# A mixture-of-experts block on one core: the fetched rows of the later tiles transposed by VectorE in 32x32 pieces

## The reference

```python
logits = jnp.einsum('bsd,ed->bse', x, router_w)
topk_vals, topk_idx = jax.lax.top_k(jax.nn.softmax(logits, axis=-1), 2)
for eid in range(8):
    w = jnp.sum(jnp.where(idx == eid, vals, 0), axis=-1)
    h = jax.nn.gelu(x_flat @ w1[eid].T, approximate=False)   # 256 -> 1024
    out = out + w[:, None] * (h @ w2[eid].T)                 # 1024 -> 256
```

## Time and profile before

| | us |
|---|---|
| time, median of 3 runs | 585.92 (585.22 to 586.15) |
| time of the profiled execution | 587.28 |
| span of the profiled execution, first to last instruction | 584.9 |
| PE busy | 521.7 (89%) |
| VectorE busy | 356.0 (61%) |
| ScalarE busy | 354.0 (61%) |
| GpSimd busy | 118.4 (20%) |

### The profile page before, as it was taken

How to read it: one execution, slowest core, us unless ns; L and a number is a source line. 1 busy time by engine, 2 the same in 40 slices (tenths; PEclk the granted TensorE clock), 3 DMA queues, 4 the chain that set the end, 5 groups by cost and what they waited for, 6 DMA issues and landing times.

```text
span 584.9 us, 10193 instructions
## 1 busy us (share of the span) xinstructions
PE 521.7 (89%) x3432; PEld 337.4 (58%) x3433; DVE 356.0 (61%) x1176; ACT 354.0 (61%) x314; POOL 118.4 (20%) x96
## 2 busy tenths in 40 slices
PE   7787879666799897989899999999899999999994
PEld 5332323102265443535454555788799999999993
DVE  4899997898875799885799986375111111111110
ACT  1679999988998988999978998241011111111110
POOL 2000000050001162501252111145222222222222
PEclk9698989777899999999989999999899999999998
DMA  4102940065212036322227533348765555555541
GB/s 128 38 0 74 422 162 1 1 194 208 83 72 82 10 115 204 114 82 91 80 79 216 179 106 94 104 152 258 220 180 181 181 180 180 180 180 180 171 95 22
DMA packets 32831, 77.47 MB, mean 132 GB/s; under 512 B 4471, under 2 KB 25591, under 8 KB 26647
## 3 DMA queue, kind: packets, MB, share of 16 engines
q1 hardware_dynamic: 24848, 67.22, 33.0%
q0 software_dynamic: 7344, 9.72, 9.0%
q10 hardware_dynamic: 599, 0.02, 0.1%
HBM read 60.65 MB, written 16.29 MB: 132 GB/s over the span
## 4 chain that ended last, share of the span: by engine, by line
PE 57%; DVE 18%; ACT 14%; DMA 4%; SPq 3%; issue 3%; POOL 0%; DVEq 0%; POOLq 0%
PE h_ps L706 19%; PE y_bank L718 19%; PE rho L671 12%; DVE hbuf L877 9%; ACT hbuf L559 8%; ACT hbuf L565 3%; PE misc L651 2%; DMA out<-x_res 2%; SPq L369 1%; PE xsT_bank L694 1%; SPq L370 1%; PE xsT_bank L660 1%; PE misc L642 1%; DVE stats L844 1%; ACT hgT L588 1%
## 5 line engine op out<-in xcount | busy, mean ns | idle before, releaser
L559 ACT ACTIVATE hbuf<-hbuf 128x2048 f32<-128x2048 f32 (+2 forms) x160 | 246.9, 1594 | 39.0 <-DVE hbuf L877 38.9
L877 DVE TENSOR_SCALAR hbuf<-featT,txtb 128x512 f32<-128x512 f32 x525 | 216.2, 480 | 19.4 <-PE rho L671 18.2
L671 PE MATMUL rho<-hbuf,wpad 128*32 128x512 f32 x1232 | 174.7, 647 | 34.7 <-ACT hbuf L565 19.8
L706 PEld LDWEIGHTS h_ps<-xsT,w_st 128*128 128x128 f32 x1280 | 151.1, 194 | 26.8 <-issue 25.2
L706 PE MATMUL h_ps<-xsT,w_st 128*128 128x128 f32 x1280 | 157.1, 280 | 1.2 <-issue 1.2
L718 PE MATMUL y_bank<-w_sb,hgT 128*128 x640 | 152.5, 389 | 2.0 <-DVE y_sb L1049 2.0
L718 PEld LDWEIGHTS y_bank<-w_sb,hgT 128*128 128x128 f32 x640 | 119.3, 193 | 38.2 <-issue 23.5
L588 ACT ACTIVATE hgT<-h_ps 128x1024 f32<-128x1024 f32 x40 | 40.8, 1021 | 165.7 <-PE h_ps L706 165.6
L510 POOL DMA_INDIRECT out<-y_sb,meta x40 | 68.4, 1711 | 302.1 <-DMA out<-y_sb,meta 128.1
L671 PEld LDWEIGHTS rho<-hbuf,wpad 128*32 128x32 f32 x1232 | 30.0, 112 | 120.8 <-ACT hbuf L565 46.1
L1035 DVE COPY xsT<-xsT_bank 128x256 f32<-128x256 f32 x40 | 16.9, 423 | 87.2 <-PE xsT_bank L694 87.2
(11 more groups left out here) (131 smaller groups left out, 189.6 us busy)
## 6 DMA issues: line engine op xcount, KB each, us to landing
w_st<-in_w SPq DMA_DIRECT2D x40, 1024.0 KB, 4.9
w_sb<-in_w SPq DMA_DIRECT2D x8, 1024.0 KB, 13.4
xs<-row_scratch SPq DMA_DIRECT2D x40, 132.5 KB, 4.5
row_scratch<-pad SPq DMA_DIRECT2D x33, 132.5 KB, 20.7
x_res<-in_x SPq DMA_DIRECT2D x4, 512.0 KB, 4.8
out<-x_res SPq DMA_DIRECT2D x4, 512.0 KB
hgT<-in_x SPq DMA_DIRECT2D x3, 512.0 KB, 4.2
out<-y_sb,meta POOLq DMA_INDIRECT x40, 6.5
```

The costliest lines, as they stand in the source:

```text
L559: ins = s.activation(h, h, ACT.Tanh)
L671: ins = t.matmul(rho[q % 2][32 * j:32 * j + 32, :], wpad[:, c, 31 - r:63 - r], hbuf[:, k % HB, j, :], start=(k == 0), stop=(last and c == ...
L706: ins = t.matmul(h_ps[:, k * P:(k + 1) * P], w1_st[:, par, c, k * P:(k + 1) * P], xsT[:, c, :], start=(c == 0), stop=(c == DC - 1))
L877: ins = v.tensor_scalar(hbuf[:, k % HB, j:j + 1, :], featT[:, c, q:q + 1, :], txtb[:, c, bb, CG * r + j:CG * r + j + 1], None, ALU.add)
```

## The change

From tile 17 on (the 18th) `turn_x` is gone from PE's order: `step` leaves it out unless a count is given, and the calls for tiles 16 and later give none. In its place `x_out` gets the count: VectorE waits for the fetched rows (xs_in) and for the end of up of the tile before (h_ps_ok), and then writes xsT by 16 transposing instructions. Each takes 32 rows and 32 columns in both halves of 128 columns, 32 partitions by 2 x 32 elements, and writes them, each 32x32 piece turned, to 32 partitions of xsT. Their outer loop goes over the input's partitions, the inner one over the output's. The last raises xsT_ok, for which up waits as before. Tiles 0 to 16 stay as they were.

```diff
-            def step(i, slot4, count, following, turned=None, late=lambda: None):
+            def step(i, slot4, count, turned=None, late=lambda: None):
...
-                if following:
+                if turned:
                     turn_x(i + 1, (slot4 + 1) % 4, turned)
...
             for i in range(16, SURE + 1):
-                step(i, i % 4, i // 2 + 1, True, (i + 1) // 4 + 1)
+                step(i, i % 4, i // 2 + 1)
...
-            def x_out(i, slot4):
-                dve.wait_ge(xsT_ps_ok, i + 1)
-                v.tensor_copy(xsT[:].rearrange("p c k -> p (c k)"), xsT_ps).then_inc(xsT_ok, 1)
+            def x_out(i, slot4, count=None):
+
+                if count is None:
+                    dve.wait_ge(xsT_ps_ok, i + 1)
+                    v.tensor_copy(xsT[:].rearrange("p c k -> p (c k)"), xsT_ps).then_inc(xsT_ok, 1)
+                else:
+                    dve.wait_ge(xs_in[slot4], 16 * count)
+                    dve.wait_ge(h_ps_ok, i)
+                    for b in range(0, P, SQ):
+                        for d in range(0, P, SQ):
+                            ins = v.transpose(xsT[d:d + SQ, :, b:b + SQ],
+                                              xs[b:b + SQ, slot4, 0:D].rearrange("p (c k) -> p c k", c=DC)[:, :, d:d + SQ])
+                    ins.then_inc(xsT_ok, 1)
...
-            x_out(17, 1)
+            x_out(17, 1, 5)
```

More of the change, by code:

```diff
@@ L334, in flamingo_moe @@
         LOOP_END = SURE + 1 + 4 * QUADS
+        SQ = 32
         block = ctx.enter_context(nc.Block())
@@ L780, in _ @@
             turn_x(14, 2, 4)
-            step(14, 2, 8, True, 4)
-            step(15, 3, 8, True, 5, late=lambda: settle("count", NQ - 1))
+            step(14, 2, 8, 4)
+            step(15, 3, 8, 5, late=lambda: settle("count", NQ - 1))
             for i in range(16, SURE + 1):
-                step(i, i % 4, i // 2 + 1, True, (i + 1) // 4 + 1)
+                step(i, i % 4, i // 2 + 1)
             with pe.Fori(0, QUADS) as n:
                 for u in range(1, 5):
-                    step(SURE + u + 4 * n, (SURE + u) % 4, 2 * n + (SURE + u) // 2 + 1, True,
-                         n + (SURE + u + 1) // 4 + 1)
+                    step(SURE + u + 4 * n, (SURE + u) % 4, 2 * n + (SURE + u) // 2 + 1)
             for i in range(LOOP_END, NT):
-                step(i, i % 4, i // 2 + 1, i < NT - 1, (i + 1) // 4 + 1)
+                step(i, i % 4, i // 2 + 1)
             e = expert(NT - 1)
@@ L1101, in _ @@
             settle("table", 3, 1)
-            x_out(17, 1)
+            x_out(17, 1, 5)
             y_out(15, 3)
-            x_out(18, 2)
+            x_out(18, 2, 5)
             y_out(16, 0)
-            x_out(19, 3)
+            x_out(19, 3, 5)
             y_out(17, 1)
-            x_out(20, 0)
+            x_out(20, 0, 6)
             y_out(18, 2)
@@ L1111, in _ @@
                 for u in range(1, 5):
-                    x_out(SURE + 1 + u + 4 * n, (SURE + 1 + u) % 4)
+                    x_out(SURE + 1 + u + 4 * n, (SURE + 1 + u) % 4, n + (SURE + 1 + u) // 4 + 1)
                     y_out(SURE - 1 + u + 4 * n, (SURE - 1 + u) % 4)
@@ L1115, in _ @@
                 if i < NT - 1:
-                    x_out(i + 1, (i + 1) % 4)
+                    x_out(i + 1, (i + 1) % 4, (i + 1) // 4 + 1)
                 y_out(i - 1, (i - 1) % 4)
```

## The result

The changed kernel takes 603.64 us (median of 4 runs, 602.4 to 604.1) against 586.03 for the kernel before in the same session: a ratio of 1.0292, 95% interval 1.0266 to 1.0318. (The ratios are estimated from the single executions; the quotient of the two medians is a little different, here 1.0300.) It is slower by some 2.9%, where 606.2 us (592 to 621) had been forecast. The profiled execution's span is 601.5 us, 16.6 more than before.

The account below looks back on a forecast made before the run. The prediction took PE's own row of work to bound the expert tiles. Twenty periods at +0.865 us (+17.3), head +3.0 and end 0 gave +20.3 on a median of 585.92: 606.2 us, range 592 to 621.

Parts of the forecast that it names:

- What bounds the stage: Back-to-back expert tiles: PE is busy throughout, 7.245 us per period; taking off 0.21 us of transposition would give 7.03.
- The chain: From up's end to the next up's end: 0.04 us to VectorE, sixteen instructions, 0.07 to PE's load, 3.84 for up.
- the formula: In the loop, a period is at least 3.95 + 16 t us, with t from one VectorE instruction to the next.
- The price t: Distance between successive VectorE transposing instructions: 0.26 us forecast, break-even at 0.206, giving 8.11 us per period.
- the bounds: For t on VectorE: 0.13 us if small instructions overlap, or whole duration plus gap, as L820's four suggest.
- the reading taken: On VectorE, each instruction starts after its predecessor ends: 0.246 us duration plus 0.014 gap, ends 0.225 and 0.294.
- The estimate from the Trainium skill's 311 ns: For one VectorE transposing instruction of 64 instead of 128 elements: 0.245 us, sum within 0.5 us of the forecast.
- The head: Tiles 17 and 18, before the 20 periods: bare sixteen, 4.8 us PE idle, 1.5 for slow clock; +3.0 us.
- The end and the other engines: After the last up nothing changes, 0 us; work behind the sixteen on VectorE comes some 4 us later without cost.
- Overlap (1): Rival on VectorE: the sixteen overlap, t = 0.13, period 7.03 us, total 581.1 us; chance 0.13.
- The additions as the pace (2): Rival on POOL: indirect additions into out, 7.30 us per cycle, set the pace; total 585.9 us; chance 0.04.
- A clock that falls in the steady stretch (3): Rival in the loop: PE's clock falls with the gaps, 1.5 us every second up, +15, 621 us; chance 0.06.

Follow-up runs that it names:

- two buffers: The change with two buffers for xsT, so the sixteen wait for the end of up one tile earlier; 584.18 us, ratio 0.9935 to the kernel before.
- The copies: The change with plain copies in place of the sixteen transposing instructions, same pairs of partitions and shapes; 585.62 us.
- the fourteen: The change with fourteen transposing instructions per tile instead of sixteen, the last two left out; 592.64 us.
- the kernel without a move: The change with all sixteen instructions reading and writing partitions 0 to 31; 585.77 us, beside 586.33 for the kernel before.
- the best version: The change with two buffers for xsT and tiles 17 to 19 transposed on TensorE; 581.21 us, ratio 0.9902 to the kernel before.

## Why the prediction was right, and where its sizes were off

*What bounds the stage.* Right: PE had no slack, and what counted was whether someone would make it wait. With the sixteen hidden (two buffers) the period came to 7.03 us, as worked out from the 0.21 us that left PE's queue.

*The chain.* Right in every link: 0.03 us from up's end to VectorE (0.04 forecast), 0.06 to PE's load (0.07), 3.84 for up. The copies and the fourteen confirm the formula at other values: 7.13 and 7.44 us.

*The price t.* 0.26 forecast, 0.249 measured; 4.16 us for sixteen against 3.99. That was worth 0.16 us per tile or 3.3 us in all, more than the 2.6 us by which 606.2 lay too high. In the span the account is 16.6 us in place of 20.3: 3.3 less in the 20 periods, 0.5 more in the head, and up of 16 earlier by 1.0, which the change doesn't touch. The choice between the bounds, which was the step on which the sign hung, was right for the reason given: L820's four instructions were the same case. The 0.127 of the kernel without a move stands at the lower bound of 0.13, and 0.249 between the 0.225 and 0.294 of the reading taken. The composition was less right. I had built the duration of 0.246 us from a copy (0.211) and 32 elements more. Measured: a moved copy lasts 0.185, a moved transposition 0.236, one that doesn't move 0.190. So a copy was shorter than I counted and transposing dearer, by 0.05 instead of 0.034; the two errors partly cancelled, and that 0.246 came so near to 0.236 is luck to that extent. The estimate from the Trainium skill's 311 ns for 128x128 bf16 ("VectorE: DVE Perf Modes", section "The three transpose paths"), 0.245 us, was as near (0.243 with the 1.07 ns per element of the earlier trace rows, which puts the sum 1 us lower and not 0.5); the trace's 0.236 decides.

*The head.* +3.0 forecast, +3.53 measured. The sixteen were shorter than counted, but the slow clock cost more: 5.94 - 3.65 = 2.3 us where I had charged 1.5. That is one execution: the kernels in which only the output or only the input moves have the same head, and there up of 17 loaded for 5.08 us, 1.4 more than 3.65, and the head cost 2.7 and 2.6 us. What I had called the cause, the sixteen of tile 17 lying bare, is not the whole of it, as the run with tile 17 on TensorE shows.

*The end and the other engines.* Right: 19.65 us against 19.60, and nothing behind the sixteen on VectorE held anyone up.

*The rivals.* Overlap (1) is refuted by the change's own trace, and the kernel without moves shows what it would have given: 0.127 us from start to start and 7.03 us per tile. The additions as the pace (2) fall with the two buffers. A clock that falls in the steady stretch (3) didn't come: 1.00 over 155 us with a gap of 1.03 us per tile.

Left open: where in a head the slow stretch falls from one execution to the next, and how long it lasts there.

## What to carry to other kernels

Before small instructions are moved to an idle engine, look for a row of that engine where consecutive ones go from one group of 32 partitions to another: whether they overlap there sets the price, here by a factor of two, and the mean busy time of the engine says nothing on it. Then write down the chain from the end of the last reader to the start of the next, and see whether the cover is long enough; where it is not, a second buffer can be worth more than faster instructions, here from 1.03 to 0.99 of the time before. An idle stretch that a fetch sets can move when something ahead of it is sped up, and the slow clock with it, as in the two traces with tile 17 alone back on TensorE.

## What the runs showed of the hardware that I had not expected

- The same transposing instruction is recorded as 0.190 us long where it overlaps its neighbours, and 0.236 where it starts after its predecessor's end; the difference is in the records of the runs without and with a move, with the same shape.
- A move of the input alone or of the output alone costs as much as both (0.246, 0.249, 0.249 us from start to start).
- After a longer idle stretch of PE the next loads are not slower in proportion. In up of 17 of the two kernels in which only the output or only the input moves, 4.68 and 4.65 us of idle were followed by 5.08 us of loads, where the change has 5.94 after the same 4.68:

```profile
404.51 5.08 PEld L707 LDWEIGHTS h_ps<-xsT,w_st 128*128 128x128 f32 x32 [4.68 <-issue]
```

```profile
405.84 5.08 PEld L707 LDWEIGHTS h_ps<-xsT,w_st 128*128 128x128 f32 x32 [4.65 <-issue]
```

In other heads 3.86 us were followed by 6.26, 4.20 by 6.08, 2.71 by 5.28. In the kernel before 2.05 us were followed by 5.01 us for loads that take 3.32 elsewhere, but in the best version the 2.41 us ahead of the same down left it at 3.32. So the length of the idle stretch alone does not tell whether, or for how long, the slow clock comes.
